# Moving the ternary weight preparation of a later feed-forward stage into the tile loop of an earlier expert stage

## The reference

```
logits = x2d @ gate_w.T;  _, sel = top_k(sigmoid(logits), 4)
a = silu(g) * u * cw.T[:, :, None];  out = einsum('eti,eih->th', a, Wd)
```

```
w = w_fp32.astype(bfloat16);  w_g = w.reshape(-1, 64)
scale = clip(mean(abs(w_g), -1), 1e-8);  q = clip(round(w_g / scale), -1, 1)
wq = w + (q * scale - w)                 # all in bf16
gu = x @ wq_gu.T;  h = silu(gate) * up;  out = rms_norm(h) @ wq_p.T
```

## Time and profile before

| what | us |
|---|---|
| median of 3 runs | 3038.7 (3037.46 to 3044.28) |
| profiled execution, its own time | 3031.64 |
| span of that execution in the trace | 3029.9 |
| tile loop of the expert stage, from its first tile load to its last copy | 1126.3 to 1401.0 |
| later feed-forward stage, from its first weight load to its last normalisation | 2060.2 to 2255.4 |

### The profile page before, as it was taken

How to read it: one execution, slowest core, us unless ns; L and a number is a source line. 1 busy time by engine, 2 the same in 40 slices (tenths; PEclk the granted TensorE clock), 3 DMA queues, 4 the chain that set the end, 5 groups by cost and what they waited for, 6 DMA issues and landing times. The chain is left out here.

```text
span 3029.9 us, 48733 instructions
## 1 busy us (share of the span) xinstructions
PE 2454.1 (81%) x16188; PEld 2151.8 (71%) x16188; DVE 1779.2 (59%) x4130; ACT 1433.1 (47%) x3786; POOL 775.5 (26%) x750
## 2 busy tenths in 40 slices
PE   4888775999999819995688888981867999995997
PEld 3666675999999819995466666661866888884675
DVE  4677666777778632222588888785644545541332
ACT  3444445777777403332665666642424555541221
POOL 0111010000000260003477776670851122111000
PEclk8878897999999759997799989995977899887999
DMA  3000003000000462223111110001000000001000
GB/s 115 0 0 0 13 0 111 1 2 2 2 2 2 125 208 90 95 93 114 55 59 41 39 35 34 38 1 42 1 27 13 1 1 0 0 0 39 1 0 28
DMA packets 78283, 108.25 MB, mean 36 GB/s; under 512 B 14970, under 2 KB 65906, under 8 KB 77060
## 3 DMA queue, kind: packets, MB, share of 16 engines
q1 hardware_dynamic: 71940, 88.93, 9.1%
q0 software_dynamic: 6144, 16.79, 1.7%
HBM read 78.29 MB, written 27.40 MB: 35 GB/s over the span
## 5 line engine op out<-in xcount | busy, mean ns | idle before, releaser
L1657 POOL TENSOR_TENSOR l2a_hb<-l2a_hb,l2a_Cb 128x1024 f32<-128x1024 f32 x128 | 303.5, 2381 | 127.5 <-DVE l2a_hb L2100 126.8
L2100 DVE TENSOR_TENSOR_SCAN l2a_hb<-l2a_dA,l2a_dB 128x1024 f32<-128x1024 f32 x128 | 288.4, 2274 | 67.2 <-PE l2a_dB L1738 39.1
L1738 PE MATMUL l2a_dB<-l2a_diag,l2a_dxT 64*128 64x128 f32 x2048 | 194.7, 312 | 71.2 <-DVE l2a_hb L2100 59.2
L1738 PEld LDWEIGHTS l2a_dB<-l2a_diag,l2a_dxT 64*128 64x128 f32 x2048 | 143.8, 199 | 137.6 <-DVE l2a_hb L2100 77.9
L1952 ACT ACTIVATE l2a_dA<-l2a_delta,l2a_An 128x255 f32<-128x255 f32 x512 | 214.1, 497 | 51.7 <-DVE l2a_delta L2033 37.1
L2714 ACT ACTIVATE l3a_ex<-l3a_sm,l3a_nm 128x128 f32<-128x128 f32 (+1 forms) x256 | 113.7, 446 | 130.4 <-DVE l3a_nm L2825 130.4
L792 PE MATMUL l1a_QK<-l1a_xh,l1a_wqkv_h 128*128 128x256 f32 x512 | 146.8, 287 | 14.6 <-DVE l1a_wo L1015 10.8
L1488 DVE TENSOR_TENSOR l1f_a<-l1f_s,l1f_GU 128x96 f32<-128x96 f32 x95 | 24.2, 255 | 225.0 <-ACT l1f_s L1376 225.0
L986 ACT ACTIVATE l1a_prh<-l1a_ex,l1a_rz 128x256 fp32r<-128x256 f32 x256 | 116.4, 502 | 72.4 <-DVE l1a_rz L1037 72.4
L1758 PE MATMUL l2a_YS<-ident,l2a_hb 128*128 128x128 f32 x1024 | 147.9, 293 | 1.0 <-POOL l2a_hb L1657 1.0
L792 PE MATMUL l1a_QK<-l1a_xh,l1a_wqkv 128*128 128x256 f32 x512 | 146.0, 285 | 0.0
(11 more groups left out here) (561 smaller groups left out, 7675.3 us busy)
## 6 DMA issues: line engine op xcount, KB each, us to landing
l2a_Cb<-c_rows SPq DMA_DIRECT2D x8, 2048.0 KB
l1f_xl<-moe_x_rows SPq DMA_DIRECT2D x95, 128.0 KB, 2.1
moe_y_rows<-l1f_yo SPq DMA_DIRECT2D x95, 128.0 KB, 1.7
l1a_raw<-in_L_attn_w_qkv_dram SPq DMA_DIRECT2D x12, 512.0 KB, 4.7
moe_x_rows<-X SPq DMA_DIRECT2D x1, 4224.0 KB, 17.4
l1f_dL<-in_L_ffn_Wd_dram SPq DMA_DIRECT2D x1, 3072.0 KB, 24.0
X<-in_L_attn_x_dram SPq DMA_DIRECT2D x8, 256.0 KB, 4.6
l1a_raw<-in_L_attn_w_o_dram SPq DMA_DIRECT2D x4, 512.0 KB, 4.1
```

What stands on the lines that cost most here:

```text
L1657: nc.gpsimd.tensor_tensor(h[:, :, :], h[:, :, :], Cb[p][:, s0:s0 + UN, :], ALU.mult).then_inc(hc_ready, 1)
L1738: last = nc.tensor.matmul(out[:, m:m + 2, j * P + a:j * P + a + HP], dxT[q][a:a + HP, j, c * P:(c + 1) * P], diag[q][a:a + HP, j, s0 + m:s ...
L2100: nc.vector.tensor_tensor_scan(flat(hb[u % RING]), flat(dA[(i * NU + u) % DAS]), dB[u % 2][:, :], 0.0, ALU.mult, ALU.add).then_inc(scanned, 1)
```

## The change

The chain that makes the ternary weights leaves `l2_ffn`. It is done in `l1_ffn`, in six chunks of 128 x 1024 numbers, eleven steps a chunk, one step in each of the rounds t = 8 to 73 of VectorE's tile loop, behind the aT copy of that round. GpSimd loads each chunk of raw weights (512 KB) into one of two buffers and stores each finished chunk (256 KB, bf16) to a DRAM tensor `l2f_ternary`. `l2_ffn` loads these 1.5 MB in three DMAs straight into `above`, and the six groups of turned blocks are copied by ScalarE (groups 0, 2, 4) and VectorE (groups 1, 3, 5) in turn. Absolute value is now max(-w, w) on VectorE, and the two comparisons w > limit and w < -limit with a subtraction take the place of comparison times sign. Four tables of the router (`lr`, `eq`, `pos`, `sel`) now lie in the two raw buffers, so the first loads wait for `back_ready`, VectorE's last operation before its tile loop.

```diff
@@ l1_ffn
-        lr = ph.sb("lr", [P, TT, E])
+        rawq = [ph.sb(f"raw{n}", [P, 4, D]) for n in range(2)]
+        lr, eq, pos, sel = (rawq[n // 2][:, n % 2 * 2:n % 2 * 2 + 2, :].rearrange("p a (t e) -> p (a t) e", e=E) for n in range(4))
+        GROUP, RC, QS = 64, 4, 11
+        QC = sh.ternary.shape[1] // RC
+        NG = RC * D // GROUP
@@ gpsimd
+            def load_raw(c):
+                if c >= 2:
+                    pool.wait_ge(quant_steps, (c - 2) * QS + 1)
...
+                nc.gpsimd.dma_start(rawq[c % 2][:, :, :], src).then_inc(raw_in[c % 2], 16)
+
             pool.wait_ge(back_ready, 1)
+            load_raw(0)
+            load_raw(1)
+            for c in range(QC):
+                if c + 2 < QC:
+                    load_raw(c + 2)
+                pool.wait_ge(quant_steps, (c + 1) * QS)
+                nc.gpsimd.dma_start(sh.ternary[:, c * RC:(c + 1) * RC, :], hat[c % 2][:, :, :]).then_inc(quant_out[c % 2], 16)
             pool.wait_ge(rows_out, 16 * TT * TOPK)
+            for n in range(2):
+                pool.wait_ge(quant_out[n], 16 * len(range(n, QC, 2)))
@@ vector
+            def quantize(dve, c, n):
+                did = c * QS + n
+                if did:
+                    dve.wait_ge(quant_steps, did)
+                if n == 0:
+                    dve.wait_ge(raw_in[c % 2], 16 * (c // 2 + 1))
+                    ins = nc.vector.tensor_copy(wb[:, :, :], rawq[c % 2][:, :, :])
+                elif n == 1:
+                    ins = nc.vector.scalar_tensor_tensor(out=mag[:, :, :], in0=wb[:, :, :], scalar=-1.0, in1=wb[:, :, :],
+                                                         op0=ALU.mult, op1=ALU.max)
+                elif n == 2:
+                    ins = nc.vector.tensor_reduce(total[:, :], groups(mag), AX_X, ALU.add)
+                elif n == 3:
+                    ins = nc.vector.tensor_scalar(scale[:, :], total[:, :], 1.0 / GROUP, 1e-8, ALU.mult, ALU.max)
+                elif n == 4:
+                    nc.vector.tensor_scalar(limit[:, 0, :], scale[:, :], 0.5 + 2.0 ** -9, None, ALU.mult)
+                    ins = nc.vector.tensor_scalar(limit[:, 1, :], scale[:, :], -(0.5 + 2.0 ** -9), None, ALU.mult)
+                elif n == 5:
+                    ins = nc.vector.tensor_tensor(groups(up), groups(wb), spread(limit[:, 0]), ALU.is_gt)
+                elif n == 6:
+                    ins = nc.vector.tensor_tensor(groups(dn), groups(wb), spread(limit[:, 1]), ALU.is_lt)
+                elif n == 7:
+                    ins = nc.vector.tensor_tensor(up[:, :, :], up[:, :, :], dn[:, :, :], ALU.subtract)
+                elif n == 8:
+                    ins = nc.vector.tensor_tensor(groups(dn), groups(up), spread(scale), ALU.mult)
+                elif n == 9:
+                    ins = nc.vector.tensor_tensor(dn[:, :, :], dn[:, :, :], wb[:, :, :], ALU.subtract)
+                else:
+                    if c >= 2:
+                        dve.wait_ge(quant_out[c % 2], 16 * (c // 2))
+                    ins = nc.vector.tensor_tensor(hat[c % 2][:, :, :], wb[:, :, :], dn[:, :, :], ALU.add)
+                ins.then_inc(quant_steps, 1)
...
+                if 8 <= t < 8 + QC * QS:
+                    quantize(dve, (t - 8) // QS, (t - 8) % QS)
@@ l2_ffn
         @block.sync
-            sp.dma_start(raw[:, 0:RT, :], w["L2_ffn_w_gate_up"].rearrange("(r p) d -> p r d", p=P)).then_inc(w_loaded, 16)
...
+            for n in range(3):
+                part = slice(n * THIRD, (n + 1) * THIRD)
+                sp.dma_start(above[:, part, :], sh.ternary[:, part, :]).then_inc(w_loaded[n], 16)
@@ tensor
-            pe.wait_ge(q_ready, 1)
             for n in range(len(TURNS) // 8):
                 if n >= 2:
-                    pe.wait_ge(w_kept, n - 1)
+                    pe.wait_ge((w_kept, w_low_kept)[n % 2], n // 2)
+                pe.wait_ge(w_loaded[n % 2 if n < 4 else 2], 16)
@@ scalar
-            nc.scalar.activation(mag[:, :, :], wb[:, :, :], ACT.Abs).then_inc(abs_ready, 1)
-            nc.scalar.activation(raw[:, :, :], wb[:, :, :], ACT.Sign).then_inc(sign_ready, 1)
-            for n in range(len(TURNS) // 8):
+            for n in range(0, len(TURNS) // 8, 2):
                 act.wait_ge(w_turned, n + 1)
+                nc.scalar.copy(turned_to(n), WT[0][:, :, :].rearrange("p m t -> p (m t)")).then_inc(w_kept, 1)
@@ vector
-            dve.wait_ge(w_loaded, 16 * (1 + KC))
-            nc.vector.tensor_copy(wb[:, :, :], raw[:, :, :]).then_inc(wb_ready, 1)
...
-            nc.vector.tensor_tensor(above[:, :, :], wb[:, :, :], mag[:, :, :], ALU.add).then_inc(q_ready, 1)
             keep_low(ph, dve, 0, xh[0], xl[0], xl_ready)
+            for n in range(1, len(TURNS) // 8, 2):
+                dve.wait_ge(w_turned, n + 1)
+                nc.vector.tensor_copy(turned_to(n), WT[1][:, :, :].rearrange("p m t -> p (m t)")).then_inc(w_low_kept, 1)
```

More of the change, by code:

```diff
@@ L30 @@
 POOL_DMA_SEMS = range(180, 186)
+QUANT_SEMS = range(190, 194)
 class Phase:
@@ L1134, in l1_ffn @@
         tau = ph.sb("tau", [P, 1])
-        lr = ph.sb("lr", [P, TT, E])
+        rawq = [ph.sb(f"raw{n}", [P, 4, D]) for n in range(2)]
+        lr, eq, pos, sel = (rawq[n // 2][:, n % 2 * 2:n % 2 * 2 + 2, :].rearrange("p a (t e) -> p (a t) e", e=E) for n in range(4))
+        assert TT * E == 2 * D
         lc = ph.sb("lc", [P, 2, NT, WIDE])
@@ L1168, in l1_ffn @@
         yo = [ph.sb(f"yo{n}", [P, D]) for n in range(YO)]
+        GROUP, RC, QS = 64, 4, 11
+        QC = sh.ternary.shape[1] // RC
+        NG = RC * D // GROUP
+        RT = w["L2_ffn_w_gate_up"].shape[0] // P
+        assert RT % RC == 0 and QC * QS <= TILES
+        wb, mag = (ph.sb(n, [P, RC, D], BF16) for n in ("wb", "mag"))
+        up, dn = (t[:, :, :].bitcast(BF16).rearrange("p j (h d) -> p (j h) d", d=D) for t in (ph.xin, ph.r))
+        hat = [ph.sb(f"hat{n}", [P, RC, D], BF16) for n in range(2)]
+        total = ph.sb("total", [P, NG])
+        scale = ph.sb("scale", [P, NG], BF16)
+        limit = ph.sb("limit", [P, 2, NG])
+        groups = lambda t: t[:, :, :].rearrange("p r (g e) -> p (r g) e", e=GROUP)
+        spread = lambda t: t[:, :, None].to_broadcast([P, NG, GROUP])
         x_rows = sh.moe_rows
@@ L2128, in l2_ffn @@
 def l2_ffn(nc, sh, w):
-    GROUP = 64
     FF = w["L2_ffn_w_proj"].shape[1]
@@ L2170, in l2_ffn, with turned_to @@
         block = ctx.enter_context(nc.Block())
-        groups = lambda t: t[:, :, :].rearrange("p r (g e) -> p (r g) e", e=GROUP)
-        spread = lambda t: t[:, :, None].to_broadcast([P, NG, GROUP])
         TURNS = [(r, kc) for kc in range(KC) for r in range(RT)]
         TURNS += [(RT + j * (FF // D) + f // KC, f % KC) for f in range(FC) for j in range(KC)]
+        def turned_to(n):
+            if n < len(TURNS) // 8 - 2:
+                return wgu[:, n * 8 // RT, n * 8 % RT * P:(n * 8 % RT + 8) * P]
+            m = n - (len(TURNS) // 8 - 2)
+            return wd[:, m * 4:m * 4 + 4, :].rearrange("p f d -> p (f d)")
         @block.sync
         def _(sp):
-            sp.dma_start(raw[:, 0:RT, :], w["L2_ffn_w_gate_up"].rearrange("(r p) d -> p r d", p=P)).then_inc(w_loaded, 16)
-            for j in range(KC):
-                n = FF // D
-                sp.dma_start(raw[:, RT + j * n:RT + (j + 1) * n, :].rearrange("p r d -> p (r d)"),
-                             w["L2_ffn_w_proj"][j * P:(j + 1) * P, :]).then_inc(w_loaded, 16)
+            for n in range(3):
+                part = slice(n * THIRD, (n + 1) * THIRD)
+                sp.dma_start(above[:, part, :], sh.ternary[:, part, :]).then_inc(w_loaded[n], 16)
         @block.gpsimd
@@ L2234, in _ @@
                 last.then_inc(w_turned, 1)
-            pe.wait_ge(w_kept, len(TURNS) // 8)
+            pe.wait_ge(w_kept, len(TURNS) // 16)
+            pe.wait_ge(w_low_kept, len(TURNS) // 16)
             def squares(k, q):
@@ L3113, in program @@
         sh.moe_y = nc.dram_tensor("moe_y_rows", (((ITEMS * SEQ * topk - experts) // P + experts) * P, D), F32).ap()
+        rows = (w["L2_ffn_w_gate_up"].shape[0] + w["L2_ffn_w_proj"].shape[0] * w["L2_ffn_w_proj"].shape[1] // D) // P
+        sh.ternary = nc.dram_tensor("l2f_ternary", (P, rows, D), BF16).ap()
         sh.moe_back = ctx.enter_context(nc.sbuf_tensor("moe_back", [P, ITEMS * NT, topk], mybir.dt.uint32))
```

53 lines of the change are left out of this document (13 added, 40 removed).

## The result

The changed kernel takes 2991.4 us (median of 4 runs, 2982.2 to 2993.8) where the kernel before took 3039.8 (4 runs, 3037.5 to 3044.3): 0.9833 of it, 95% interval 0.9809 to 0.9857. The predicted time was 2991.2. The profiled execution took 2990.45, with a span of 2988.7; before, these were 3031.64 and 3029.9. So the two traces are only 41.2 us apart, 7 us less than the medians, and the reader should ask where these 7 us are.

What follows compares the result with a forecast made beforehand. TensorE was taken to set the expert tile loop, and an unhidden weight chain the later feed-forward stage's start. Gain 49.0 less 1.0 (loop start) and 0.5 (clock) gives 47.5 us, median 3038.7 to 2991.2; range 2982 to 3002.

Steps and rivals of the forecast that it cites:

- The chain that goes: Later feed-forward stage's start: three loads, six transpose groups and copies replace the weight chain; gain 49.0 us, 46.8 to 51.3.
- rival D: Later feed-forward stage's start: loads come from DRAM much later, 3 to 4 us less gain, 2995 us; chance 0.05.
- The eleven steps: Expert tile loop: VectorE steps of at most 1.23 us fit its 2.03 us idle per round; 57 us in all, cost 0.
- the room of a step: Expert tile loop: a step may last 2.03 + 1.7 = 3.7 us before TensorE sees it.
- rival B: Expert tile loop: steps don't fit their rounds, deciding from a 4.4 us average; 3051 us at 4.6; chance 0.03.
- DMAs in the loop: Expert tile loop: six loads and six stores added on GpSimd's queue, 3.1 us of tile slack against 1.4; cost 0.
- The loop's start: Expert tile loop's start: both first raw loads go straight into the first tile loads; loss 1.0 us, bounds 0 and 2.8.
- The clock at the stage's start: Later feed-forward stage: TensorE's clock rises 6 us after work begins, before the first product; loss 0.5 us, at most 3.
- rival C: Later feed-forward stage's start: transposes with holes don't bring the clock up; 3 us less gain, 2994 us; chance 0.07.
- Transposes and the clock: Later feed-forward stage's start: the earlier trace showed full clock after only transposes, against the skill's rule.
- Sum: Whole kernel: 49.0 - 1.0 - 0.5 = 47.5 us less, median from 3038.7 to 2991.2.
- The profiled execution 7 us below the median: Kernel before: profiled run lies 7 us below the median, so the median after can come out up to 7 us lower.

Runs made afterwards that it cites:

- e1: The whole changed expert stage (steps, raw loads, stores) with the later feed-forward stage of the kernel before; 3037.1 us, 0.9983 of before.
- e4: Changed kernel with two more VectorE operations of 1.22 us behind ten of the eleven steps, on scratch nobody reads; 0.9974 of before.
- e3: Changed kernel with one more VectorE operation of 1.22 us behind ten of the eleven steps, on scratch nobody reads; 0.9778 of before.
- e9: Changed kernel with the split of the six copies undone, ScalarE alone emptying both PSUM banks; 2981.1 us.
- e8: Changed kernel with GpSimd holding back all 64 scatters until the last item's indices are there; 3010.2 us.
- e10: Changed kernel with filler transposes of the identity in TensorE's holes at the later feed-forward stage's start; 2976.1 us, 0.9818 of before.
- c1: The kernel before, unchanged, run again for a second trace; 3046.6 us.
- c2: The changed kernel, unchanged, run again; 2989.3 us, 0.9828 of before.
- e5: Changed kernel with the ten expert weight loads spread over the router, each after the first awaiting one more item's indices; 2996.9 us, 0.9857 of before.
- e6: Changed kernel with ternary weights loaded to SBUF at the end of the stage before and turned through four PSUM banks; 2980.7 us, 0.982 of before.

## Why the prediction was right, step by step

- **The chain that goes** (49.0, bounds 46.8 to 51.3): 49.7. The late chain is the predicted one, groups 1, 3 and 5 through VectorE at 1.23 us. Parts 0 and 1 were turned 4.1 and 5.3 us after the issue, 4.4 and 5.8 were taken, so rival D is out. From there it took 6.7 us to the first product, for 6.8 in the sum.
- **The eleven steps** (0.69, 1.23, 0.2; cost 0): 0.68, 1.21 and 0.16, cost 0 by e1. VectorE was 49.6 us busier over the loop, where 57 were added up: durations overlap, as said at e4. Right in result, wrong in one reason: the room of a step is not 3.7 us but 2.03 on average (e3, e4). So rival B decided from 2.03 + 0.72 = 2.75 us, not from 4.4. With steps of 0.84 us on average (9.3 us a chunk, 9.6 predicted) that changed nothing; it would have from some three times that on.
- **DMAs in the loop** (0): no wait of TensorE for any tile after the first two. Slowest tile landing 4.8 us, 3.9 before.
- **The loop's start** (1.0, bounds 0 to 2.8): 0.85 in e9, by the predicted mechanism, and 0 in after, where the stall made `back_ready` late. That it was "long there" holds only in the traces without a stall. An equal share of the engines would have delayed the first tile by 0.35 us; it was turned 4.03 us after its load against 2.31, 1.7 late, of which 0.85 reach the first product. By the Trainium skill, DMA: Bandwidth & Descriptors, section Queues, rings and completion order, an engine takes turns between its queues packet by packet; the loss that the prediction worked out from it, nearer 0.4, was too low here. The runs don't show how the engines shared. The step says nothing of the clock, and in these four traces the loop lost another 0.5 to 1.6 us; whether the raw loads cause that is open.
- **The clock at the stage's start** (0.5, at most 3): 1.1 in after, mis-sized and by another way. The prediction asked only when the clock rises; it rose in time, and fell again behind 1.4 us without work. By execution it is 0 (e4) to 1.4 us (e8: 11.67 us to the eighth `a`). A clock that stays down, as rival C had it, is what e8 shows; that the holes cause it isn't shown, since e4 has the same holes. From the first product to the next stage it took 134.5 us in before and 133.6 in after, so the rest of the stage, for whose falls of the clock the prediction left 3 us either way, gave back 2.0.
- **Transposes and the clock:** by the Trainium skill, TensorE: Matmul & The Clock Gate, section Part 4: PE-mode transpose, they don't bring the full clock. e10 has 0.99 at 2072 with nothing but transposes behind it since 2068.84, so here they do; only in e8 they didn't.
- **Sum:** predicted 47.5. Measured in the medians 48.4. That the two agree to 1 us is partly luck: the stage gives 50.6 us between the traces of before and after and 46.4 between those of c1 and c2, and no trace has the changed kernel to the letter without a stall, so that the 1.4 to 2.5 us of the loop's start come from kernels beside it.
- **The profiled execution 7 us below the median:** the prediction noted it and had no cause. The likely cause is the router's stall, 6 to 9 us there and up to 7.8 in the loop: before's one other trace, c1, has it and took 3046.6 us. The runs behind the median have no traces.

## What to carry to other kernels

Work that runs alone at a stage's start pays in full when it moves under a loop that another engine fills; what decides is the mover's average length against the idle time of a round, and slack further down the pipeline counts once. A load that follows directly on the last transfer of a chain lands in the first transfer of the next. Before a difference between two traces is explained, take a second trace of each: here the first pair differed by 8 us in a stage that the change hardly touches. The same holds for an effect seen in one trace: the clock at the start of one and the same stage took three courses in seven traces.

## What the runs showed that was not expected

- VectorE stood for up to 23.0 us and ScalarE for up to 26.2 us at a time in the router, though what they need in the program was done (1054.9 and 1075.80 above). Nine traces have it and five don't; the kernels of one chip are alike in it. Full DMA engines are not what it takes (e5); the scatters were neither shown nor cleared (e8 had no stall to remove).
- Behind 6.5 us of transposes with holes, 1.4 us without work were followed by three microseconds of half clock, in five of seven traces of the same code. With 28 filler transposes it didn't come in one trace, and in one trace without them it didn't either.
- Stages that no edit touches differ by up to 15 us between executions ("rest", 758.5 to 773.5), more than most edits here are worth. Only windows and timelines of the edited stretch could tell e6, e9 and e10 apart.
